# A DLRM tower in fp32: fifteen instead of five tables looked up by one-hot matmuls, and the interactions packed in four chunks

## What is computed

```python
e = stack([tbl_n[ids[:, n]] for n in range(26)], axis=1)       # [512, 26, 128]
combined = concatenate([dense[:, None, :], e], axis=1)         # [512, 27, 128]
inter = einsum('bfd,bgd->bfg', combined, combined)[:, iu, ju]  # 351 pairs a sample
h = concatenate([dense, inter, dense], axis=1)                 # [512, 607]
h = maximum(h @ W_top1 + b_top1, 0)                            # 512 units
h = maximum(h @ W_top2 + b_top2, 0)                            # 256 units
y = h @ W_top3                                                 # [512, 1]
```

## Time and profile before

| | us |
|---|---|
| median of 3 runs | 151.44 |
| lowest, highest | 149.96, 152.02 |
| span of the profiled execution, first to last instruction | 152.9 |

### The profile page before, as it was taken

One profiled execution on the slowest core, in us unless ns is written; L12 is line 12 of the kernel. 1 busy time (PEld: TensorE's weight loads), 2 busy tenths in 40 slices (PEclk: granted clock), 3 DMA queues, 4 the chain that ended last, 5 costly groups with the idle time before them and its releaser, 6 DMA issues.

```text
span 152.9 us, 3980 instructions
## 1 busy us (share of the span) xinstructions
PE 115.3 (75%) x1789; PEld 95.1 (62%) x1789; DVE 51.1 (33%) x88; ACT 49.8 (33%) x98; POOL 83.9 (55%) x91
## 2 busy tenths in 40 slices
PE   0339401999379965599899899958999949995993
PEld 0127201677157654486788788647989739994691
DVE  6665600076457810712103800234500405104100
ACT  5045203368499840703000800204500106104011
POOL 4777777777787877777777777777710000000000
PEclk9999955569978999557999999997799996999659
DMA  1684447999644322221222221122210000000000
GB/s 43 151 192 164 166 164 227 270 248 238 172 166 167 119 53 57 50 57 51 55 53 56 58 51 51 51 56 56 60 30 0 0 9 0 4 4 0 4 0 1
DMA packets 5547, 12.82 MB, mean 84 GB/s; under 512 B 2025, under 2 KB 3049, under 8 KB 5277
## 3 DMA queue, kind: packets, MB, share of 16 engines
q0 software_dynamic: 2688, 5.51, 15.2%
q1 hardware_dynamic: 2832, 7.05, 15.0%
q10 hardware_dynamic: 10, 0.01, 0.0%
HBM read 12.56 MB, written 0.00 MB: 82 GB/s over the span
## 4 chain that ended last, share of the span: by engine, by line
PE 57%; DMA 25%; DVE 7%; issue 7%; ACT 2%; SPq 1%; ACTq 0%
DMA table_sb<-tbl 25%; PE h_ps L539 17%; PE gram_ps L511 9%; PE h_ps L563 7%; PE h_ps L534 6%; PE fill_ps L485 5%; DVE zT L391 5%; PE gram_ps L462 3%; PE gram_ps L539 3%; PE gram_ps L464 3%; DVE featT L385 2%; ACT featT L301 1%; PE gram_ps L534 1%; PE h_ps L573 1%; DVE h L396 1%
## 5 line engine op out<-in xcount | busy, mean ns | idle before, releaser
L289 POOL DMA_INDIRECT gathered<-tbl,ids_sb x84 | 83.1, 989 | 26.9 <-issue 25.3
L539 PE MATMUL h_ps<-zT,w_inter_sb 122*128 122x128 f32 (+1 forms) x196 | 29.2, 295 | 1.6 <-DVE zT L391 1.6
L539 PEld LDWEIGHTS h_ps<-zT,w_inter_sb 122*128 122x128 f32 (+1 forms) x196 | 27.3, 203 | 4.7 <-DVE zT L391 1.9
L462 PE MATMUL gram_ps<-onehot,table_hi 125*128 125x512 f32 x40 | 20.8, 519 | 4.8 <-DVE table_lo L424 4.7
L314 ACT ACTIVATE zT<-gram_ps 26x224 f32<-26x224 f32 (+4 forms) x40 | 12.1, 302 | 37.7 <-PE gram_ps L511 36.9
L418 DVE TENSOR_TENSOR onehot<-h_ps,rowno 125x1536 fp32r<-125x1536 f32 x10 | 17.5, 1755 | 17.8 <-PE gram_ps L464 16.9
L511 PE MATMUL gram_ps<-featT 128*26 128x26 f32 (+2 forms) x1280 | 15.5, 188 | 9.0 <-issue 5.8
L391 DVE COPY zT<-gram_ps 26x224 f32<-26x224 f32 (+4 forms) x40 | 12.9, 323 | 24.6 <-PE gram_ps L511 23.5
L511 PEld LDWEIGHTS gram_ps<-featT 128*26 128x26 f32 (+1 forms) x1280 | 13.2, 102 | 11.9 <-issue 7.5
L464 PE MATMUL gram_ps<-onehot,table_lo 125*128 125x512 f32 x40 | 19.6, 490 | 0.0
L307 ACT ACTIVATE featT<-fill_ps 128x512 f32<-128x512 f32 (+1 forms) x14 | 9.1, 656 | 26.4 <-PE fill_ps L485 26.4
(11 more groups left out here) (33 smaller groups left out, 55.5 us busy)
## 6 DMA issues: line engine op xcount, KB each, us to landing
table_sb<-tbl SPq DMA_DIRECT2D x5, 500.0 KB
w_inter_sb<-w_inter SPq DMA_DIRECT2D x1, 1792.0 KB, 29.9
gathered<-tbl,ids_sb POOLq DMA_INDIRECT x84, 3.8
oh_ids_sb<-oh_ids SPq DMA_DIRECT2D x1, 1000.0 KB
w_dense_sb<-w_dense SPq DMA_DIRECT2D x1, 512.0 KB, 25.0
w_sb<-w SPq DMA_DIRECT2D x1, 512.0 KB, 26.8
dense_sb<-dense SPq DMA_DIRECT2D x1, 256.0 KB, 23.2
oh_ids_sb<-oh_ids SPq DMA_DIRECT2D x1, 250.0 KB
```

The lines of the kernel that those rows point to most:

```text
L289: pool.indirect_dma_start(out=gathered[:, t, pos - GATHERED[0], :], out_offset=None, in_=tables[table], in_offset=bass.IndirectOffsetOnAxi ...
L462: nc.tensor.matmul(lookup_ps(k), table_hi[:, k % 2, rows], onehot[:, c, :], start=(c == 0), stop=False)
L539: last = nc.tensor.matmul(layer1_ps(t, n), w_inter_sb[0:k, c, units], zT[0:k, c, tile], start=False, stop=(c == CHUNKS - 1), skip_group_ch ...
```

## The change

- Fifteen tables are looked up by one-hot matmuls; eleven are gathered (44 indirect DMAs). The host pads each one-hot table to 128 partitions x 8 chunks (twelve tables) or x 10 chunks (three), 126 chunks in all.
- The ids of a table come by a broadcast DMA into `ids_all`, where ACT writes ids + 1 beside them (`next_ids`). DVE then compares both with one row number in one `tensor_scalar` (`compare_two`), two chunks at once; ACT makes two chunks of every second table (L411), the three of ten chunks among them. In a table's turn DVE computes the low part ahead of the compares. Onehot buffers are two, split buffers three.
- Gather number n (from the sixth on) waits until TensorE has done 3 (n - 4) chunks. `gathered` has three tile buffers in place of four.
- A sample has 32 slots in `featT` in place of 27, some of them copies of others (`COPIED`). ACT copies two tables' lookups at once (`pair_to_featT`) to slots that lie in one group of four. The dense field is also kept apart, contiguous (`denseT`).
- Each product matmul is 32 x 27, each tile one stage, and `zT` has four chunks of 128 partitions, filled by 8 copies a quarter of a tile (32 copies of 128 elements a tile, in two engines). Layer 1 is four matmuls and one dense. The order of TensorE's work after the lookups is written out by hand, products in quarters between other work.

```diff
-ONEHOT_TABLES = (0, 1, 3, 6, 8)
+ONEHOT_TABLES = (0, 1, 3, 6, 7, 8, 11, 12, 13, 14, 21, 15, 16, 18, 20)
+LARGER = (7, 13, 21)
+SHORT, LONG = 8, 10
+GATHERS_AHEAD = 4
+CHUNKS_A_GATHER = 3
+ZCHUNKS = 4
...
+def chunks_ahead(n):
+    return min((n - GATHERS_AHEAD) * CHUNKS_A_GATHER, row_chunks_to(ONEHOTS))
...
+                        if n > GATHERS_AHEAD:
+                            pool.wait_ge(chunk_done, chunks_ahead(n))
...
+            def compare_last(k):
...
+                if k >= 2:
+                    act.wait_ge(lookup_done, k - 1)
+                for c in range(dve_chunks(k), row_chunks(k)):
+                    nc.scalar.activation(onehot[k % 2][:, c, :], ids_all[:, k % IDS_BUFS, 1, :], ACT.Abs,
+                                         bias=row_number(minus_rowno, k, c)).then_inc(id_off_ready, 1)
+                act.wait_ge(id_off_ready, act_chunks_to(k + 1))
+                act_part = onehot[k % 2][:, dve_chunks(k):row_chunks(k), :]
+                nc.scalar.activation(act_part, act_part.bitcast(fp32), ACT.Relu, bias=1.0, scale=-1.0) \
...
+            def next_ids(k):
+                act.wait_ge(ids_all_in[k % IDS_BUFS], ids_loads(k))
+                nc.scalar.activation(ids_all[:, k % IDS_BUFS, 0, :], ids_all[:, k % IDS_BUFS, 1, :], ACT.Relu, bias=1.0) \
+                    .then_inc(next_ids_ready, 1)
...
+            def compare_two(k, c):
+                nc.vector.tensor_scalar(onehot[k % 2][:, c:c + 2, :], ids_all[:, k % IDS_BUFS, :, :],
+                                        row_number(rowno, k, c + 1), None, ALU.is_equal).then_inc(onehot_dve, 2)
...
             for k in range(ONEHOTS):
...
+                if k > 0:
+                    low_parts(k)
+                    dve.wait_ge(next_ids_ready, k)
+                else:
+                    dve.wait_ge(ids_0_ready, 1)
+                if k >= 2:
+                    dve.wait_ge(lookup_done, k - 1)
```

More of the change, by code:

```diff
@@ L50 @@
[L50 to L82, removed]
@@ L85, in groups_of_stage @@
[L85 to L96, removed]
+LAST = TILES - 1
+ONEHOT_TABLES = (0, 1, 3, 6, 7, 8, 11, 12, 13, 14, 21, 15, 16, 18, 20)
+LARGER = (7, 13, 21)
+ONEHOTS = len(ONEHOT_TABLES)
+SHORT, LONG = 8, 10
+FIRST = SHORT // 2 * DIM
@@ new lines, in buffer_chunks, with dve_chunks, dve_chunks_to, act_chunks_to @@
+def buffer_chunks(buffer, buffers):
+    return max(row_chunks(k) for k in range(buffer, ONEHOTS, buffers))
+def dve_chunks(k):
+    if row_chunks(k) == LONG:
+        return LONG - 2
+    return SHORT if k > 0 and k % 2 == 1 else SHORT - 2
+def dve_chunks_to(k):
+    return sum(dve_chunks(n) for n in range(k))
+def chunks_ahead(n):
+    return min((n - GATHERS_AHEAD) * CHUNKS_A_GATHER, row_chunks_to(ONEHOTS))
+def act_chunks_to(k):
+    return row_chunks_to(k) - dve_chunks_to(k)
+def quads(cols):
+    a, b, c, d = cols
+    if a + d == b + c:
+        return a, c - a, b - a
+    raise ValueError(cols)
@@ L97, in tower @@
+def tower(nc, dense, ids, oh_ids, tables, w_inter, w_dense, small, w2, out):
     fp32, fp32r, i32 = mybir.dt.float32, mybir.dt.float32r, mybir.dt.int32
@@ L119, in tower @@
[L119 to L122, removed]
-        dense_sb = sb("dense_sb", [P, TILES, DIM])
[L124 to L127, removed]
+        rowno_i = sb("rowno_i", [P, SHORT + LONG], i32)
@@ L248, in load_table @@
             def load_table(k):
[L249 to L253, removed]
+                if k >= RAW_BUFS:
+                    sp.wait_ge(hi_ready, 2 * (k - RAW_BUFS + 1))
+                    sp.wait_ge(lo_ready, 2 * (k - RAW_BUFS + 1))
@@ new lines, in lookup @@
+                if k > 0:
+                    pe.wait_ge(hi_ready, 2 * (k + 1))
+                    pe.wait_ge(lo_ready, 2 * (k + 1))
+                for c in range(row_chunks(k)):
+                    rows = slice(c * DIM, (c + 1) * DIM)
+                    if k == 0 and c * DIM % FIRST == 0:
+                        pe.wait_ge(hi_ready, c * DIM // FIRST + 1)
+                        pe.wait_ge(lo_ready, c * DIM // FIRST + 1)
+                    if c < dve_chunks(k):
+                        pe.wait_ge(onehot_dve, dve_chunks_to(k) + c + 1)
+                    else:
+                        pe.wait_ge(onehot_act, act_chunks_to(k + 1))
+                    nc.tensor.matmul(lookup_ps(k), table_hi[k % SPLIT_BUFS][:, rows], onehot[k % 2][:, c, :],
+                                     start=(c == 0), stop=False).then_inc(chunk_done, 1)
+                    last = nc.tensor.matmul(lookup_ps(k), table_lo[k % SPLIT_BUFS][:, rows], onehot[k % 2][:, c, :],
+                                            start=False, stop=(c == row_chunks(k) - 1))
@@ L527, in layer1 @@
[L527 to L541 removed]
+                    pe.wait_ge(denseT_ready, 1)
@@ L542, in layer1 @@
                     last.then_inc(h1_psum, 1)
-            def layer1_before(stage):
-                layer1_start(stage)
-                for n in range(N1 - BESIDE[stage]):
-                    layer1(stage, n)
+                elif n == N1 - 1:
+                    last.then_inc(h1_psum_last, 1)
             def layer2(t):
@@ L566, in layer2 @@
-                last.then_inc(h2_psum, 1)
-            def layer3(t):
-                if t == 0:
-                    pe.wait_ge(small_in, 48)
-                pe.wait_ge(h2_ready, N2 * (t + 1))
+                pe.wait_ge(h1_ready, N1 * (t + 1))
+                for n in range(N2):
+                    for k in range(N1):
+                        last = nc.tensor.matmul(layer2_ps(t, n), w2_sb[:, k, n * P:(n + 1) * P],
+                                                h1[:, t % 2, k, :], start=(n == 0 and k == 0), stop=(k == N1 - 1),
+                                                skip_group_check=True)
@@ new lines, in layer2, with layer2_last @@
+                last.then_inc(h2_psum, 1)
+            def layer2_last(half):
+                if half == 0:
+                    pe.wait_ge(h2_ready, N2 * LAST)
+                    pe.wait_ge(h1_ready, N1 * LAST + N1 // 2)
+                else:
+                    pe.wait_ge(h1_act, N1 // 2)
+                for n in range(N2):
+                    for k in range(half * N1 // 2, (half + 1) * N1 // 2):
+                        last = nc.tensor.matmul(layer2_ps(LAST, n), w2_sb[:, k, n * P:(n + 1) * P],
+                                                h1[:, LAST % 2, k, :], start=(k == 0), stop=(k == N1 - 1))
+                    if half == 1:
+                        last.then_inc(h2_psum, 1)
@@ new lines, in _ @@
+            fill(1, 0)
+            products(0, 0)
+            products(0, 1)
+            layer1_dense(1)
+            fill(1, 1)
+            fill(1, 2)
+            products(0, 2)
+            fill(2, 0)
+            products(0, 3)
+            fill(2, 1)
+            fill(2, 2)
+            products(1, 0)
+            layer1_dense(0)
+            products(1, 1)
+            fill(3, 0)
+            fill(3, 1)
+            products(1, 2)
+            layer1(0, 0)
+            products(1, 3)
@@ new lines, in _ @@
+            layer1(0, 1)
+            products(2, 0)
+            layer1(0, 2)
+            layer1(0, 3)
+            products(2, 1)
+            fill(3, 2)
+            products(2, 2)
+            layer1(1, 0)
+            layer1(1, 1)
+            products(2, 3)
+            layer2(0)
+            products(LAST, 0)
+            layer1(1, 2)
+            products(LAST, 1)
+            layer1(1, 3)
+            layer1_dense(LAST)
+            products(LAST, 2)
+            layer1_dense(2)
+            products(LAST, 3)
@@ new lines, in _ @@
+            layer1(2, 0)
+            layer1(2, 1)
+            layer1(2, 2)
+            layer2(1)
+            layer1(2, 3)
+            layer1(LAST, 0)
+            layer1(LAST, 1)
+            layer2(2)
+            layer1(LAST, 2)
+            layer1(LAST, 3)
+            layer2_last(0)
+            layer2_last(1)
+            layer3(0, LAST)
+            layer3(LAST, 1)
+def first_layer_layout(w1):
+    w = np.zeros((P, ZCHUNKS, HID1), w1.dtype)
+    placed = set()
+    for q in range(4):
+        for c in range(ZCHUNKS):
+            for r in range(QUAD):
+                column = ABOVE[q][c] if r < CUT[q] else BELOW[q][c]
+                other = r if r < FEATS else COPIED[r - FEATS]
+                lo, hi = sorted((FIELD_AT[column], FIELD_AT[other]))
+                if lo != hi and (lo, hi) not in placed:
+                    placed.add((lo, hi))
+                    pair = lo * FEATS - lo * (lo + 1) // 2 + (hi - lo - 1)
+                    w[QUAD * q + r, c] = w1[DIM + pair]
+    assert len(placed) == FEATS * (FEATS - 1) // 2
```

635 lines of the change are left out of this document (350 added, 285 removed).

## The result

The changed kernel took **122.59 us** (120.85 to 123.93) against 151.73 (149.96 to 153.2) for the kernel before beside it: 0.803 of it, 95% interval 0.789 to 0.816. Forecast were 131 in a range of 119 to 148, and faster with a chance of 0.83. The profiled execution took 120.85 us, with a span of 118.4; the forecast span was 132.

The account below looks back on a forecast made before the run. TensorE, ACT and DVE were to end the lookups within 2 us of each other; DVE's 71.3 plus 5 of waits gave 76, plus a 56 us second stage 132 of span, times 0.99 131 us, range 119 to 148.

Parts of the forecast that it names:

- nothing collides: Rival, chance 0.15: TensorE sets the lookup stage, second stage loses only 3 us; span 121, time 119.5 us.
- T 70: T is when products start, ending the lookup stage; 70 us in the rival without collisions, 76 in the forecast.
- The likeliest case: The forecast itself, whole kernel: 131 us, its own range 124 to 140, chance 0.60.
- TensorE alone to 69.6: Lookup stage: first lookup at about 7 us plus 62.6 us of TensorE's work, ending at 69.6.
- DVE's 66.3 us of work and 5 us for waits: Lookup stage: DVE's compares and low parts from 5 us end at 71.3; 5 for buffer waits puts products at 76.
- Shut out: Rival, chance 0.07, lookup stage: compares stand still 0.82 us at each gather; products start at 107, time 161 us.
- Gathers in time: Lookup stage: 44 gathers take 57 us, or 73 at 1.65 each, so paced gathers delay nothing needed.
- Loads: Lookup stage: 15.5 MB in 70 us, 221 GB/s, keeps up; rival, chance 0.06: 165 GB/s, products at 96, 150.5 us.
- Second stage, 48.1 us of bare work: After the lookups: TensorE's own full-clock time for products, layers 1 to 3 and transposes, 48.1 us.
- 8 us around it: Second stage losses: half clock 3, gaps 2, late copies 1.1, end 1.9; together 8, making the stage 56 us.
- The factor 0.99: Whole kernel: the earlier span stood 1.0% above the median, so 132 us of span became 131 us.
- the 2 us taken for it in the sum: Start of the lookups: TensorE's sum allowed 2 us for one slow stretch.

Follow-up runs that it names:

- The padded kernel before: The kernel before the change with its five tables padded from 1000 to 1024 rows, run twice: 218.5 and 218.47 us, ratios 0.964 and 0.968.
- strided: Changed kernel with layer 1's dense matmuls reading every 32nd element of `featT` instead of contiguous `denseT`: 130.61 us.
- seven chunks: Changed kernel with seven chunk matmuls per layer-1 block instead of four, chunks 0 to 2 added twice: 138.61 us.

## Why the prediction was right, and where it was off

The direction and the split were right: a first stage longer, a second shorter by more. The sizes were nearest to the rival that was given 0.15, *nothing collides* (T 70, second stage 51, 119.5 us). The likeliest case, 124 to 140 us, just missed. Step by step:

- **TensorE alone to 69.6, first product at 70.59.** The end was right within 1 us, by two errors that nearly cancel: the first lookup began at 5.90, not 7, and from there it took 64.7 us, not 62.6, with 1.5 of waits for compares in it. Nothing but that term was left.
- **DVE's 66.3 us of work and 5 us for waits: this step failed.** The compare was taken at the rate of the memset, 0.87; it is 0.69 in a row, which over 52 of them is 9 of the 10 us. DVE was busy 56.22 us from 5 to 70.6, ACT 54.21 instead of 64.2: `next_ids` took 0.62 instead of 0.72, pair copies 1.16 instead of 1.3, and 6.6 us are overlap that the sum counted twice (high parts of 1.04 us start 0.95 before the next instruction). With 9 us of slack the buffers absorbed nearly all the hand-overs. The sum added the waits to DVE's work as if DVE were the bound; the engine that was the bound waited 1.5 us for compares. The Trainium skill ("VectorE: DVE Perf Modes", Mode 2×_2P) has two elements a cycle for such an operation, from which the prediction estimated 0.6 us: the trace, at 0.69, agrees better with that than with 0.87.
- **Shut out: DVE no, POOL yes.** Compares took 0.732 to 0.815 us with POOL busy beside them for 45.58 of 65.6 us, so DVE never stood still for a gather, which was the costly half of that rival. The other half is there: gathers wait for compares to end (last heading). The prediction took its low part as a sign of the rule on two-port modes; that operation has two inputs, and at 1.22 us it was no test of it.
- **Gathers in time: yes.** The last starts at 72.80. They took 1.13 on average, against a forecast of up to 1.65, and as before a gather waits out the low part beside it (13.02 is 0.82 after 12.20):

```profile
10.97 1.23 DVE L535 TENSOR_TENSOR table_lo<-table_sb,table_hi 128x1024 fp32r<-128x1024 f32 x1 [2.37 <-ACT table_hi L428]
11.13 1.89 POOL L342 DMA_INDIRECT gathered<-tbl,ids_sb  x1 [0.46 <-PE gram_ps L614]
12.12 2.74 DVE L529 TENSOR_SCALAR onehot<-ids_all,rowno 128x1024 fp32r<-128x1024 int32 x4
```

- **Loads: right**, 249 GB/s over the lookups, above the 221 forecast, and what they hang on is shown by the run over 125 partitions.
- **Second stage, 48.1 us of bare work: 45.1 busy.** Layer 1 20.1 in the chain (20.2 forecast), products 12.0 (13.6), layer 2 7.4 (8.1), transposes 3.8 (4.2), layer 3 1.8 (2.0).
- **8 us around it: this step failed too**, 2.7 measured. Half clock was put at 3 us and came to none; gaps and waits were put at 3.1 and came to 0.9; the end was put at 1.9 and is 1.8 behind 116.56. The z copies were covered: TensorE never waits for them. The forecast took gaps and half clock from the kernel before, where the pieces were whole; on the slower chips whole pieces bring them back.
- **The factor 0.99** was the wrong way round: it set one execution's span beside the median time of others, and a run is 2.2 to 2.5 us longer than its own span here (120.85 and 118.4). So the time was missed by 8.4 us where the profiled span was missed by 13.6 and the median span (120.25) by 11.8. That the time came nearer than the span is luck.

## What to carry to other kernels

When the bound engine's own work is summed, the other engines' work is compared with it, and waits are added only to the engine that is really last: slack of 9 us or more in two of three engines absorbed nearly all hand-overs here. Make the outer size of a load 128 even if rows must be padded; three partitions of 128 decided 33 us. Put other work between long runs of tiny matmuls (some 8 us on a slower chip; not measured on the first kind), and try both forms of a tensor operation: a compare with a per-partition scalar ran 1.7 times as fast as one with two tensors (0.69 and 1.16 us in a row).

## What the runs showed of the hardware

- **TensorE's instructions come late for tens of microseconds, on two of three chips.** The padded kernel before, on such a chip (chain, then a stretch of 50 us):

```profile
107.53 0.20 PE gram_ps L511
107.73 2.60 issue
110.33 0.20 PE gram_ps L511
110.53 2.60 issue
```

```profile
60.00:110.00 50.00, 2.82 (x42) 1.77 (x43) 0.47 (x1) 1.84 (x2) 37.76 (x41) 0.50 0.20 53
```

One product each 2.8 us, with no semaphore to wait for; its last gather starts at 109.98, and from 121.53 products come 163 in 2.37 us. The same kernel on the other such chip has lookups in that stretch, and they wait instead, 57.6 us in seven waits; its first product stands at 122.99, and its last gather starts at 109.90. So in both the late instructions end within 15 us of the last gather. But gathers alone do not make them: on the first chip the last gather of the kernel before starts at 110.39, and its products wait for late instructions only 5.8 us, in three gaps. In the changed kernel's relatives on the slower chips, most gathers lie beside lookups, which wait 0.2 us (whole products, strided) or 1.7 (seven chunks) for late instructions; there it happens from 71 to 76 us, beside the last gathers, for 3 to 4 us in all. The cause was not tried and stays open. What the change would be worth on such a chip can be estimated: some 100 us (226.7 to about 128).
- **A gather waits for the DVE instruction beside it, of either form; no compare was seen to wait for a gather.** With DVE idle a gather takes 0.94 us. Beside the first compare of a table:

```profile
44.90 0.74 DVE L529 TENSOR_SCALAR onehot<-ids_all,rowno 128x1024 fp32r<-128x1024 int32 x1
45.01 1.45 POOL L342 DMA_INDIRECT gathered<-tbl,ids_sb  x1 [0.35 <-PE gram_ps L614]
```

The compare ends at 45.64 and the gather at 46.46, 0.82 later, as behind a low part. Of the changed kernel's 44 gathers 34 took 0.98 us or more, and 30 of these end 0.82 us, to 0.03, after a DVE instruction that ran beside them. Eighteen take only 1.01 to 1.04, as the compare has little left to run when they start. Two-input compares last longer and cost more: with them gathers took 1.69 us on average, with one-input compares 1.13. The Trainium skill ("SBUF — State Buffer", Who interferes with whom) has it that a DVE operation in a two-port mode and a GpSimd operation shut each other out for a whole instruction. The trace agrees for the gather, by the 0.82; that DVE waits for a gather no run here shows, with no compare over 0.815 us.
- **The granted clock of the first 10 us reads 1.00** while the lookups from 6.46 to 10.30 start 0.43 us apart; from 10.69 on it is 0.23. The row does not show this half-speed stretch. Ten lookups at 0.20 more are the 2 us taken for it in the sum.
